# Channel statistics of four image pairs on ScalarE, a later mean over the groups, and a reordered fifth quad in a routed-convolution kernel

## The chip, the cores and the metric

The kernel runs on one core of a Trainium2 chip. The metric is the device time of one execution in microseconds (us), lower is better. The core has TensorE (PE in the profile; its weight loads are PEld), VectorE (DVE), ScalarE (ACT), GpSimd (POOL) and SyncE (SP), which here only issues DMAs. Every engine works through its own instructions in the order in which they are written and waits for the others at semaphores.

## The reference

The input is 32 images of 32 x 32 pixels with 64 channels. Cut to what matters:

```
h = group_norm(x)                          # 32 groups: two channels and all pixels
repeat 3 times:                            # STEPS
    k, v     = h Wk, h Wv                  # two heads of 16
    attn     = softmax over the pixels of (q . k) / 4, per head
    logits   = (sum over pixels of attn * v) Wmlp      # one logit for each of 4 experts
    weights  = softmax(masked logits / 1.5)
    wsel     = the two largest weights, normalised     # the rest are zero
    h_mod    = h * (1 + mean over heads of attn * 1024 * softplus(alpha))
    h        = sum over e of wsel[e] * (conv3x3(h_mod, We[e]) + be[e])
    mask     = without the expert chosen first (the last one stays allowed)
x = x + h
x = x + involution(group_norm(x))          # second layer
```

Since a convolution is linear, the kernel first mixes the experts' weights of an image by `wsel` and then runs one convolution per image.

## The kernel before, in words

Two images stand on the 128 partitions (2 x 64 channels); such a pair is `k`, 0 to 15. Pairs are worked on in **quads** of two pairs, four images: quad `q` = 4p + j, where `p` is the **phase**, 0 to 5, and `j` is 0 to 3. A phase is one step for one half of the batch: phases 0, 2, 4 hold pairs 0 to 7, phases 1, 3, 5 pairs 8 to 15. A quad is convolved in two halves `h` of 16 rows, each with nine taps `t` (`convolve`, L760), four small matmuls a tap; the trace has two records for each of them, 72 a half. From quad 4 on every second quad is **short**: `convolve_short` (L729) works on sums and differences of rows, in four stages of three column taps (24 records a stage). Beside the taps PE runs small jobs at fixed places, by `beside` and `beside_short`: attention maps (L610), scores and values (L552), logits (L598), the permutation of mask and bias (L621), transposes of the input (L523) and `group_average` (L535), a product with `pair_avg` that averages the two channels of a group.

`att` has two units in PSUM. The list `ATT_USES` gives the order of their uses; a use may only start when the use before it in the same unit has been read (`claim`).

**First phase.** Input pairs are transposed into `xin`. VectorE takes the statistics of each (`turned_stats`, L1437 and L1438), `group_average` the mean over a group, `chunk_norm` (L1176 to L1181) the variance, GpSimd the inverse root (L1701, L1704), ScalarE the normalised pair (`normalise`, L913). Chunk 2 is pairs 8 to 11, chunk 3 is pairs 12 to 15; they are not used before phase 1. On GpSimd `row_forms` (L1721 to L1728) follows chunk 3.

**A quad's work beside PE.** ScalarE begins the mixing of the weights (`begin_combine`, L952), VectorE adds the other experts (`combine`, L1402), multiplies the image by 1 + map (`modulate`, L1318), and for a short quad makes row sums (`sum_rows`, L1354 and L1356) and differences (`subtract_rows`, L1370), later the middle rows (`middle_rows`, L1378 and L1379) and the finished rows (`finish_rows`, L1386). ScalarE takes other quads' results out of PSUM (`empty_conv`, L961).

**From quad 6 on** (`GATHER_FROM`) only the two chosen experts are used. `pick_experts` on VectorE (phase 1) or `route_beside` on GpSimd (phases 2 and on) writes their numbers, `top_at`, and signals `top_ready`. SP then loads eight numbers into registers (`chosen_of`, L443) and issues eight DMAs that fetch the two experts of each of the four images (`gather`, L458). `begin_combine(6)` on ScalarE waits for these, `combine_two(6)` (L1423) on VectorE for it. Behind `begin_combine(6)` on ScalarE stands `route_exp(2)` (L924), which starts `route_beside(2)` on GpSimd. Its numbers are for `gather(8)`. Behind `begin_combine(8)` stand the last roundings of the attention of phase 2 (`round_attention`, L988), without which the map of quad 8 can't be made.

`row_max` (L1190), the exponentials (L919) and `weigh` (L1199) are the attention's softmax on VectorE, ScalarE and VectorE. `weigh` reads both units of `att` and so frees the second for the next map.

Of the kernel before, what the change touches and what calls it, by code (L numbers as in the profile page):

```python
# [11 lines left out]
ALU = mybir.AluOpType  # L12
# [4 lines left out]
S = H * W  # L17
# [31 lines left out]
def att_uses():  # L49

    uses = [(0, ("gn", 0)), (0, ("scores", 0)), (1, ("values", 0)), (0, ("logits", 0))]

    def attention_map(q):
        return [(0, ("map", q, 0)), (1, ("map", q, 1))]

    uses += attention_map(0)
    uses += [(0, ("permute", 0))] + [(1, ("turn", 13)), (1, ("turn", 14)), (1, ("turn", 15)), (0, ("gn", 2))]
    uses += attention_map(1) + [(1, ("gn", 3))] + attention_map(2) + attention_map(3) + [(0, ("scores", 1)), (1, ("values", 1))]
    uses += [(0, ("logits", 1))] + attention_map(4)
    for p in range(1, PHASES - 1):  # L60
# [74 lines left out]
def build(nc, A, out):  # L135
    ctx = ExitStack()
    with ctx:
# [3 lines left out]
        def sem(name):  # L141
            return ctx.enter_context(nc.semaphore(name))
# [141 lines left out]
        residual_added = sem("residual_added")  # L284
        final_emptied = sem("final_emptied")
        mv_ready = sem("mv_ready")
        late_mean = sem("late_mean")
        late_mv_ready = sem("late_mv_ready")
        pads_zeroed = sem("pads_zeroed")
# [207 lines left out]
        def _(eng):  # L497
# [150 lines left out]
            def beside(p, j, h, t):  # L648
                at = (j, h, t)
                q = QP * p + j  # L650
                if p == 0:
                    if at == (0, 0, 4):
                        permute(0)
                    elif at in ((0, 0, 3), (0, 0, 5), (0, 0, 7)):
                        turn(12 + t // 2)
                    elif at == (0, 1, 4):
                        group_average(2, chunk(2), CH, mv_ready, 12)
                    elif at == (0, 1, 5):
                        attention_map(1)
                    elif at == (1, 0, 5):  # L660
                        group_average(3, chunk(3), CH, mv_ready, 16)
                    elif at == (1, 1, 2):
                        attention_map(2)
                    elif at == (2, 0, 2):
                        attention_map(3)
                    elif at == (2, 0, 6):
                        attend(1, "scores", sw)
                        attend(1, "values", uw)
                    elif at == (2, 1, 7):
                        logits(1)  # L670
                    elif at == (3, 1, 2):
                        attention_map(4)
# [191 lines left out]

            eng.wait_ge(misc_free, 4)
            eng.wait_ge(late_mv_ready, GP + QP)
            eng.wait_ge(mv_ready, NP + QP)
            nc.tensor.matmul(att[:, 1, 0:2 * GP], pair_avg[:, :], mv[:, GP:NP, :], start=True, stop=True)\
                .then_inc(misc_full, 1)
            for k in range(1, NP):  # L870
# [13 lines left out]
        def _(eng):  # L884
# [92 lines left out]
            def round_attention(p, n):  # L977
# [9 lines left out]
                    eng.wait_ge(reduced, 2 * (p - 1) + n)  # L987
                nc.scalar.activation(parts[:, :], attn[:, :], ACT.Copy).then_inc(parts_ready if n == 2 else rounded, 1)  # L988

            def late_stats(q, n):  # L990

                k, before = slot(q, n), 2 * (q - QP * LAST) + n
                if q in SHORT:
                    eng.wait_ge(residual_added, residuals(q))
                else:
                    eng.wait_ge(final_emptied, final_parts(q, 1))
                part = stats[:, k, 0, 0:1]
                nc.scalar.activation(unused, xin[:, k, :], ACT.Copy, scale=1.0 / (32 * S), accum_out=part).then_inc(late_mean, 1)
                eng.wait_ge(late_mean, before + 1)
                nc.scalar.activation(mv[:, k, 0:1], part, ACT.Copy, scale=32.0)  # L1000
                nc.scalar.activation(unused, xin[:, k, :], ACT.Square, scale=-1.0 / 32, bias=part, accum_out=mv[:, k, 1:2])\
                    .then_inc(late_mv_ready, 1)
                eng.wait_ge(late_mv_ready, before + 1)

            def expanded_weights():

# [28 lines left out]
            for k in (13, 14, 15):  # L1035
                turned(k)
            empty_conv(0, 0)
            normalise(2)
            empty_conv(0, 1)
            begin_combine(2)  # L1040
            empty_conv(1, 0)
            normalise(3)
            empty_conv(1, 1)
# [117 lines left out]
        def _(eng):  # L1161
# [180 lines left out]
                        v.scalar_tensor_tensor(comb[:, 0, n, cols], experts[:, e, cols], wsel[:, 0, QP * n, e:e + 1],  # L1342
                                               comb[:, 0, n, cols], ALU.mult, ALU.add).then_inc(comb_added[n], 1)

            def sum_rows(q):

                w = SHORT.index(q)
                pads = xpad[:, 2 * (q % 2):2 * (q % 2) + 2, :, :]
                modulated(eng, q)
                if w:  # L1350
                    eng.wait_ge(middle_full, 2 * w)
                else:
                    eng.wait_ge(forms_out, 16 * FORMS_WRITTEN)
                v.tensor_tensor(row_sums[:, 0, :, :, :], pads[:, :, 1:H + 1:2, :], pads[:, :, 2:H + 2:2, :], ALU.add)\  # L1354
                    .then_inc(sums_ready, 1)
                v.tensor_tensor(row_sums[:, 1, :, :, :], pads[:, :, 2:H + 2:2, :], pads[:, :, 1:H + 1:2, :], ALU.subtract)\  # L1356
                    .then_inc(sums_ready, 1)

            def subtract_rows(q):

# [29 lines left out]
                eng.wait_ge(rounded, 2 * (p - 1) + n + 1)  # L1390
                v.scalar_tensor_tensor(attn[:, :], parts[:, :], below[:, n:n + 1], attn[:, :], ALU.mult, ALU.add).then_inc(reduced, 1)

            def combine(q):
                p, j = divmod(q, QP)
                cols = slice(0, 4 * ROW if q in SHORT else TAPS * C)
                for e in range(1, K):
                    for n in range(2):
                        if e > 1:
                            eng.wait_ge(comb_added[n], (K - 1) * (2 + q) + e - 1)
# [158 lines left out]
            combine(1)  # L1558
            turned_stats(9)
            turned_stats(10)  # L1560
            turned_stats(11)
            chunk_norm(2)
            eng.wait_ge(norm_done, GP)
            modulate(1)
            turned_stats(12)
            turned_stats(13)
            turned_stats(14)
            turned_stats(15)
            chunk_norm(3)
            combine(2)  # L1570
            modulate(2)
# [6 lines left out]
            shift_logits(1)  # L1578
            reduce_attention(1, 0)
            route(1)  # L1580
            next_mask_and_bias(1)
            reduce_attention(1, 1)
            combine(4)
            modulate(4)
            sum_rows(4)
            permuted(1)
            subtract_rows(4)
            pick_experts(1)

            for p in range(1, PHASES):  # L1590
                for j in range(QP):
# [17 lines left out]
                    if q + 1 < QUADS:  # L1609
# [2 lines left out]
                            shift_logits(p + 1)  # L1612
                        if q == QP:
                            row_max(p + 1)
                        (combine_two if q + 1 >= GATHER_FROM else combine)(q + 1)
                        if j == 0 and attended:
                            if q > QP:
                                row_max(p + 1)
                            weigh(p + 1)
                        if q in SHORT:  # L1620
                            ahead = (0,) if j == 0 or q == QUADS - 2 else (0, 1)
                            modulate(q + 1, ahead)
# [1 line left out]
                            if ahead == (0,):  # L1624
                                modulate(q + 1, (1,))
                            finish_rows(q, 0)
                        if j == 3 and attended:
                            reduce_attention(p + 1, 1)
                            permuted(p + 1)
# [269 lines left out]
```

## Time and profile before

| | us |
|---|---|
| median of 3 runs | 656.03 (655.46 to 656.08) |
| the profiled execution | 655.59 |
| its span, first to last instruction | 653.8 |
| PE busy | 625.2 (96%) |
| DVE busy | 519.5 (79%) |
| ACT busy | 331.1 (51%) |
| POOL busy | 179.3 (27%) |

The profile is of one execution. All starts in the text are us from the start of its span; what lies around the span is 655.59 - 653.8 = 1.8 us. A row of the timeline has start, duration, engine, line, operation, tiles and count; in brackets stands how long the engine was idle before it and what ended that. Several instructions of one line are merged in a row, and its duration then is from the first's start to the last's end. The granted clock of TensorE (PEclk) is a share of its full speed; its mean over the span is 0.982.

### The profile page before, as it was taken

The page shows a single profiled execution, that of the slowest core. Times are in us where ns is not written, and L with a number is a line of the kernel's source. Part 1 is how long each engine was busy: PE and PEld are TensorE (multiplying, and loading weights), DVE is VectorE, ACT ScalarE, POOL GpSimd, SP SyncE. Part 2 cuts the span into 40 slices and gives each one's busy share as a digit, 9 for nine tenths or more (in the row PEclk, how much of TensorE's full clock was granted, in tenths as well). Part 3 has the DMA queues.
Part 4 walks back from the last instruction along what each step waited for, and adds up shares of the span by engine and source line. Part 5 has one row for each costly group of instructions (what it writes and reads, how often), then busy time and mean ns, then how long its engine had stood idle before and what let it go on. Part 6 is the DMA issues. An engine that isn't in the chain of part 4 may idle for free.

```text
span 653.8 us, 15424 instructions
## 1 busy us (share of the span) xinstructions
PE 625.2 (96%) x5984; PEld 257.1 (39%) x5984; DVE 519.5 (79%) x812; ACT 331.1 (51%) x455; POOL 179.3 (27%) x193
## 2 busy tenths in 40 slices
PE   6869999999999999999999999999999999999995
PEld 6533333323343333333333434333444444444442
DVE  5689874998666776775788899869888988888885
ACT  3755443412342143234214756735777887787761
POOL 2100250005500730081028003413432342243230
PEclk9989899999999999999999999998999999999998
DMA  9940030024424243326412642000122221312222
GB/s 323 223 79 2 1 81 7 1 62 109 98 75 97 74 101 94 74 73 151 106 35 66 155 112 74 2 9 10 41 50 56 59 49 41 73 42 49 51 64 65
DMA packets 67461, 47.95 MB, mean 73 GB/s; under 512 B 53602, under 2 KB 54596, under 8 KB 67396
## 3 DMA queue, kind: packets, MB, share of 16 engines
q1 hardware_dynamic: 67108, 46.82, 29.3%
q8 instruction: 47, 0.77, 0.5%
q10 hardware_dynamic: 288, 0.21, 0.1%
q14 instruction: 18, 0.15, 0.1%
HBM read 35.15 MB, written 9.76 MB: 69 GB/s over the span
## 4 chain that ended last, share of the span: by engine, by line
PE 74%; DVE 5%; issue 1%; ACT 0%; DVEq 0%; ACTq 0%
PE conv L760 23%; PE conv L729 14%; PE conv L815 12%; PE att L831 12%; PE att L552 4%; PE att L631 3%; PE att L643 2%; PE att L802 2%; PE att L610 1%; DVE x L1660 1%; DVE xpad L1370 1%; DVE comb L1423 1%; DVE xin L1432 0%; DVE xpad L1318 0%; DVE row_sums L1354 0%
## 5 line engine op out<-in xcount | busy, mean ns | idle before, releaser
L760 PE MATMUL conv<-xpad,comb 64*64 64x512 f32 x2016 | 228.0, 596 | 0.1
L1660 DVE TENSOR_TENSOR x<-conv,x 128x512 f32<-128x512 f32 x288 | 177.9, 683 | 24.1 <-PE conv L815 22.8
L760 PEld LDWEIGHTS conv<-xpad,comb 64*64 64x64 f32 x2016 | 81.6, 134 | 123.9 <-issue 120.5
L815 PE MATMUL conv<-rstack,wse 98*128 98x512 f32 x288 | 95.7, 438 | 1.7 <-DVE xin L1432 0.9
L831 PE MATMUL att<-x,cmp 64*32 64x512 f32 x1280 | 80.5, 601 | 0.0
L815 PEld LDWEIGHTS conv<-rstack,wse 98*128 98x128 f32 x288 | 48.6, 190 | 70.6 <-DVE x L1660 63.9
L1318 DVE SCALAR_TENSOR_TENSOR xpad<-att,x 128x1024 f32<-128x1024 f32 x46 | 54.6, 1218 | 24.2 <-PE att L610 24.0
L961 ACT ACTIVATE x<-conv,bias 128x512 f32<-128x512 f32 x40 | 25.3, 682 | 82.8 <-PE conv L760 82.8
L1812 POOL TENSOR_TENSOR x<-x,xin 128x1024 f32<-128x1024 f32 x15 | 35.9, 2396 | 111.5 <-ACT x L1116 111.5
L952 ACT ACTIVATE comb<-experts,small 128x768 f32<-128x768 f32 (+1 forms) x33 | 27.5, 859 | 77.1 <-PE conv L729 46.8
L729 PE MATMUL conv<-xpad,comb 64*64 64x512 f32 x480 | 56.3, 598 | 1.3 <-DVE x L1379 1.3
L1739 POOL TENSOR_TENSOR rt<-rt 128x16 f32<-128x16 f32 x12 | 5.0, 421 | 190.4 <-ACT rt L924 189.8
L729 PE MATMUL conv<-row_sums,comb 64*64 64x512 f32 x480 | 56.3, 590 | 0.5 <-DVE row_sums L1354 0.5
L1094 ACT ACTIVATE x<-att,small 64x512 f32<-64x512 f32 x64 | 44.1, 689 | 9.5 <-PE att L643 8.9
L1805 POOL TENSOR_TENSOR rstack<-x,rstack 32x1024 fp32r<-32x1024 f32 x16 | 38.2, 2386 | 23.3 <-ACT rstack L1108 23.3
L1116 ACT ACTIVATE x<-att 64x512 f32<-64x512 f32 x60 | 35.6, 593 | 15.1 <-PE att L831 14.0
L1423 DVE SCALAR_TENSOR_TENSOR comb<-experts,small,comb 128x768 f32<-128x768 f32 (+1 forms) x36 | 33.4, 952 | 5.5 <-ACT comb L952 5.3
L729 PEld LDWEIGHTS conv<-xpad,comb 64*64 64x64 f32 x480 | 18.9, 131 | 36.0 <-issue 36.0
L1386 DVE TENSOR_TENSOR x<-x,conv 128x1024 f32<-128x1024 f32 x20 | 24.4, 1218 | 10.6 <-PE conv L729 10.6
L831 PEld LDWEIGHTS att<-x,cmp 64*32 64x32 f32 x1280 | 18.6, 106 | 32.9 <-issue 30.5
L1123 ACT ACTIVATE comb<-att 128x1024 f32<-128x1024 f32 x15 | 15.4, 1027 | 31.0 <-PE att L802 31.0
L729 PEld LDWEIGHTS conv<-row_sums,comb 64*64 64x64 f32 x480 | 18.7, 133 | 30.2 <-issue 28.5
(210 smaller groups left out, 754.1 us busy)
## 6 DMA issues: line engine op xcount, KB each, us to landing
experts<-forms SPq DMA_DIRECT2D x72, 192.0 KB, 3.9
experts<-forms SPq DMA_DIRECT2D x72, 144.0 KB, 2.9
x<-in_x SPq DMA_DIRECT2D x32, 256.0 KB, 5.3
out<-comb SPq DMA_DIRECT2D x30, 256.0 KB, 3.2
rstack<-rstack SPq DMA_DIRECT2D x16, 128.0 KB, 2.3
experts<-in_We SPq DMA_DIRECT2D x1, 1152.0 KB
forms<-experts SPq DMA_DIRECT2D x2, 576.0 KB, 5.7
out<-comb SPq DMA_DIRECT2D x4, 128.0 KB, 2.2
```

Of the source, the lines that this page charges most:

```text
L729: last = nc.tensor.matmul(conv[own[to], h, HW * rows:HW * rows + HW], comb[own[rows], q % 2, n, form * ROW + kw * C:form * ROW + kw * C + ...
L760: last = nc.tensor.matmul(conv[own[to], h, HW * rows:HW * rows + HW], comb[own[rows], q % 2, n, tap(t)], xpad[own[rows], 2 * (q % 2) + n, ...
L815: nc.tensor.matmul(conv[:, unit, cols], wse[:, ORDER[i], :], rstk[s][0:RR, cols], start=True, stop=True).then_inc(exp_full, 1)
L831: last = nc.tensor.matmul(att[q, 0, bank], sum_sel[own_rows, t + upper, :], prod[i][own_rows, cols], start=(r == 0), stop=(r == len(ROUNDS ...
L952: nc.scalar.activation(comb[:, q % 2, n, cols], first, ACT.Identity, scale=weight).then_inc(comb_begun[n], 1)
L1094: done = nc.scalar.activation(xip[s][own[n], 1 + 16 * h:17 + 16 * h, 1:W + 1], att[rows, 1, bank].rearrange("p (a b) -> p a b", b=W), ACT. ...
L1116: nc.scalar.activation(fin[64 * n:64 * n + 64, cols], att[rows, 0, bank], ACT.Copy)\
L1318: v.scalar_tensor_tensor(inner(q, n), img(att[:, use.unit, :]), 1.0, img(x[:, slot(q, n), :]), ALU.add, ALU.mult).then_inc(att_free[use.un ...
L1423: v.scalar_tensor_tensor(comb[:, q % 2, n, cols], chosen[:, n, 1, cols], weight(n, 1), comb[:, q % 2, n, cols], ALU.mult, ALU.add).then_in ...
L1660: v.tensor_tensor(img(prod[i])[:, rows, :], img(conv[:, unit, :])[:, rows, :], xip[s][:, kh + 16 * h:kh + 16 * h + 16, kw:kw + W], ALU.mul ...
L1805: v.tensor_tensor(rstk[s][32:64, :], r64[32:64, :], rstk[s][32:64, :].bitcast(F32), ALU.subtract)\
L1812: v.tensor_tensor(fin, fin, xin[:, k, :], ALU.add).then_inc(fin_ready, 1)
```

## The change

In the first phase the statistics of pairs 12 to 15 move from VectorE to ScalarE (`early_stats`, with a helper that `late_stats` now uses as well), between `empty_conv(0, 0)` and `empty_conv(0, 1)`; the averages of chunk 2 move on PE from tap 4 of quad 0's second half to tap 1 of quad 1; the map of quad 1 comes one tap earlier and no longer stands behind them; on VectorE `modulate(1)` goes ahead of the statistics of pair 11, and on ScalarE `normalise(2)` behind `begin_combine(2)`.

Around the fifth quad (quad 4, the first of phase 1) the next mask and bias go between the two row sums; `weigh(2)` goes behind the first expert's additions of `combine(5)`, in place of behind all three; and `pick_experts(1)` goes from ahead of the quad to behind `finish_rows(4, 0)`.

```diff
@@ att_uses
-    uses += [(0, ("permute", 0))] + [(1, ("turn", 13)), (1, ("turn", 14)), (1, ("turn", 15)), (0, ("gn", 2))]
-    uses += attention_map(1) + [(1, ("gn", 3))] + attention_map(2) + attention_map(3) + [(0, ("scores", 1)), (1, ("values", 1))]
+    uses += [(0, ("permute", 0))] + [(1, ("turn", 13)), (1, ("turn", 14)), (1, ("turn", 15))]
+    uses += attention_map(1) + [(0, ("gn", 2)), (1, ("gn", 3))] + attention_map(2) + attention_map(3) + [(0, ("scores", 1)), (1, ("values", 1))]
@@ tensor, beside
-                    elif at == (0, 1, 4):
+                    elif at == (0, 1, 3):
+                        attention_map(1)
+                    elif at == (1, 0, 1):
                         group_average(2, chunk(2), CH, mv_ready, 12)
-                    elif at == (0, 1, 5):
-                        attention_map(1)
                     elif at == (1, 0, 5):
-                        group_average(3, chunk(3), CH, mv_ready, 16)
+                        group_average(3, chunk(3), CH, early_mv_ready, CH)
@@ scalar
+            def statistics(k, scratch, mean, done, before):
+                part = stats[:, k, 0, 0:1]
+                nc.scalar.activation(scratch, xin[:, k, :], ACT.Copy, scale=1.0 / (32 * S), accum_out=part).then_inc(mean, 1)
+                eng.wait_ge(mean, before + 1)
+                nc.scalar.activation(mv[:, k, 0:1], part, ACT.Copy, scale=32.0)
+                nc.scalar.activation(scratch, xin[:, k, :], ACT.Square, scale=-1.0 / 32, bias=part, accum_out=mv[:, k, 1:2])\
+                    .then_inc(done, 1)
+                eng.wait_ge(done, before + 1)
...
             empty_conv(0, 0)
-            normalise(2)
+            for k in range(NP)[chunk(3)]:
+                early_stats(k)
             empty_conv(0, 1)
             begin_combine(2)
+            normalise(2)
@@ vector, first phase
             turned_stats(10)
+            eng.wait_ge(norm_done, GP)
+            modulate(1)
             turned_stats(11)
             chunk_norm(2)
-            eng.wait_ge(norm_done, GP)
-            modulate(1)
-            turned_stats(12)
-            turned_stats(13)
-            turned_stats(14)
-            turned_stats(15)
             chunk_norm(3)
@@ vector, before quad 4
-            next_mask_and_bias(1)
             reduce_attention(1, 1)
             combine(4)
             modulate(4)
-            sum_rows(4)
+            sum_rows(4, (0,))
+            next_mask_and_bias(1)
+            sum_rows(4, (1,))
             permuted(1)
             subtract_rows(4)
-            pick_experts(1)
@@ vector, the loop over quads
                         if q == QP:
                             row_max(p + 1)
-                        (combine_two if q + 1 >= GATHER_FROM else combine)(q + 1)
-                        if j == 0 and attended:
-                            if q > QP:
+                            combine(q + 1, (1, 2))
+                            weigh(p + 1)
+                            combine(q + 1, (2, K))
+                        else:
+                            (combine_two if q + 1 >= GATHER_FROM else combine)(q + 1)
+                            if j == 0 and attended:
                                 row_max(p + 1)
-                            weigh(p + 1)
+                                weigh(p + 1)
...
                             finish_rows(q, 0)
+                            if q == QP:
+                                pick_experts(p)
```

TensorE in quad 0 and quad 1, before (L535 is the average of a chunk, L610 a map, L760 the convolution's taps, four instructions each):

```order
L760 MATMUL conv<-xpad,comb 64x512 x24
L535 MATMUL att<-mv,wide 128x8
L760 MATMUL conv<-xpad,comb 64x512 x4
L610 MATMUL att<-parts,map_sel 64x512 x8
L760 MATMUL conv<-xpad,comb 64x512 x36
L535 MATMUL att<-mv,wide 128x8
L760 MATMUL conv<-xpad,comb 64x512 x24
```

The same place on TensorE now (the lines have moved by two, L537 for L535 and so on):

```order
L762 MATMUL conv<-xpad,comb 64x512 x20
L612 MATMUL att<-parts,map_sel 64x512 x8
L762 MATMUL conv<-xpad,comb 64x512 x28
L537 MATMUL att<-mv,wide 128x8
L762 MATMUL conv<-xpad,comb 64x512 x16
L537 MATMUL att<-mv,wide 128x8
L762 MATMUL conv<-xpad,comb 64x512 x24
```

The map of quad 1 has moved ahead of the first average, and this average stands 28 instructions later, in quad 1.

VectorE at quad 4 before, from the choice of experts (L1289 to L1296, `small` holds `top_at` and the weights) to the first middle rows (L1378):

```order
L1289 TENSOR_SCALAR cmp<-rt 128x8x4
L1290 TENSOR_SCALAR cmp<-rt 128x8x4
L1291 TENSOR_TENSOR cmp<-cmp,small 128x8x8
L1292 TENSOR_TENSOR cmp<-cmp 128x8x2x2
L1293 TENSOR_TENSOR small<-cmp 128x16
L1295 TENSOR_TENSOR cmp<-cmp,wsel 128x8x8
L1296 TENSOR_REDUCE small<-cmp 128x16
L1190 TENSOR_REDUCE soft<-att 128x1
L1191 TENSOR_SCALAR soft<-soft 128x1
L1402 SCALAR_TENSOR_TENSOR comb<-experts,wsel,comb 128x576 x6
L1199 SCALAR_TENSOR_TENSOR att,soft<-attn,att 128x1024
```

VectorE now, from the additions of two experts (L1419 is L1402 of before, L1215 is L1199, L1334 is L1318, L1395 is L1378, L1403 is L1386, L1305 to L1312 are L1289 to L1296):

```order
L1334 SCALAR_TENSOR_TENSOR xpad<-att,x 128x32x32
L1395 TENSOR_TENSOR x<-x,conv 128x2x16x32
L1396 TENSOR_TENSOR x<-x,conv 128x2x16x32
L1334 SCALAR_TENSOR_TENSOR xpad<-att,x 128x32x32
L1403 TENSOR_TENSOR x<-x,conv 128x2x16x32
L1305 TENSOR_SCALAR cmp<-rt 128x8x4
L1306 TENSOR_SCALAR cmp<-rt 128x8x4
L1307 TENSOR_TENSOR cmp<-cmp,small 128x8x8
L1308 TENSOR_TENSOR cmp<-cmp 128x8x2x2
L1309 TENSOR_TENSOR small<-cmp 128x16
L1311 TENSOR_TENSOR cmp<-cmp,wsel 128x8x8
L1312 TENSOR_REDUCE small<-cmp 128x16
```

The choice of experts now stands behind the middle rows, a modulation and the first finished rows of quad 4.

## Rows read from the trace of the kernel before

**Rows 1.** The page's chain of work that ended last, by engine.
```profile
PE 74%; DVE 5%; issue 1%; ACT 0%; DVEq 0%; ACTq 0%
```

**Rows 2.** Timeline of PE, quads 0 and 1: start, duration, engine, line, count.
```profile
58.45 5.38 PE L760 MATMUL conv<-xpad,comb 64*64 64x512 f32 x48
66.30 0.36 PE L535 MATMUL att<-mv,wide 128*128 128x8 f32 x2 [2.46 <-DVE mv L1438]
```

**Rows 3.** Stretch 67 to 70.5: length, PE busy (count), PEclk, DMA share, GB/s.
```profile
67.00:70.50 3.50, 3.50 (x28) 0.51 0.00 0
```

**Rows 4.** Timeline of DVE, quads 0 to 2.
```profile
61.43 1.42 DVE L1437 BATCH_NORM_STATS2 stats<-xin 128x6 f32<-128x512 f32 x2
...
79.05 7.60 DVE L1402 SCALAR_TENSOR_TENSOR comb<-experts,wsel,comb 128x576 f32<-128x576 f32 x6
86.57 2.34 DVE L1318 SCALAR_TENSOR_TENSOR xpad<-att,x 128x1024 f32<-128x1024 f32 x2
```

**Rows 5.** Timeline of ACT: emptying quad 0, and two pairs' late statistics.
```profile
59.61 1.27 ACT L961 ACTIVATE x<-conv,bias 128x512 f32<-128x512 f32 x2
...
381.81 1.06 ACT L998 ACTIVATE x<-xin 128x1024 f32<-128x1024 f32 x1
...
384.36 1.06 ACT L998 ACTIVATE x<-xin 128x1024 f32<-128x1024 f32 x1
```

**Rows 6.** Timeline of PE, quad 4: values, and the map of quad 5.
```profile
134.24 3.62 PE L552 MATMUL att<-x,uw 128*32 128x512 f32 x32
...
142.19 0.63 PE L610 MATMUL att<-parts,map_sel 64*64 64x512 bf16 x8 [1.60 <-issue]
```

**Rows 7.** Timeline of DVE, quad 4.
```profile
133.71 0.18 DVE L1289 TENSOR_SCALAR cmp<-rt 128x32 f32<-128x32 f32 x1
...
136.43 4.45 DVE L1402 SCALAR_TENSOR_TENSOR comb<-experts,wsel,comb 128x576 f32<-128x576 f32 x6
140.81 1.22 DVE L1199 SCALAR_TENSOR_TENSOR att<-attn,att 128x1024 f32<-128x1024 f32 x1
...
144.59 1.22 DVE L1378 TENSOR_TENSOR x<-x,conv 128x1024 f32<-128x1024 f32 x1 [0.44 <-PE conv L729]
...
148.12 1.21 DVE L1386 TENSOR_TENSOR x<-x,conv 128x1024 f32<-128x1024 f32 x1
```

**Rows 8.** SP's register loads (duration ns, first and last start), 130 to 142.
```profile
L443 SPq TENSOR_LOAD <-small x8: 273/356/467, 134.8 to 139.4; - x8
```

**Rows 9.** Timeline of SP: the DMAs of `gather(6)` and of `gather(8)`.
```profile
141.56 5.61 SPq L458 DMA_DIRECT2D experts<-forms  x8
...
171.35 5.04 SPq L458 DMA_DIRECT2D experts<-forms  x8
```

**Rows 10.** Timeline of ACT, quads 5 and 7.
```profile
150.00 2.01 ACT L952 ACTIVATE comb<-experts,small 128x768 f32<-128x768 f32 x2 [8.88 <-PE conv L729]
153.15 0.23 ACT L924 ACTIVATE rt<-rt 128x32 f32<-128x32 f32 x1 [1.13 <-DVE rt L1245]
...
180.70 0.94 ACT L952 ACTIVATE comb<-experts,small 128x768 f32<-128x768 f32 x1 [2.39 <-DMA experts<-forms]
...
183.94 1.06 ACT L988 ACTIVATE parts<-attn 128x1024 bf16<-128x1024 f32 x1 [1.35 <-DVE attn L1391]
```

**Rows 11.** Timeline of POOL: `top_at` of phase 2.
```profile
165.86 0.20 POOL L1767 CAST small<-cmp 128x16 int32<-128x16 f32 x1
```

**Rows 12.** Timeline of PE: starts of quad 6, of quad 8's map, of quad 8.
```profile
166.15 1.89 PE L729 MATMUL conv<-row_sums,comb 64*64 64x512 f32 x16
...
187.53 0.64 PE L610 MATMUL att<-parts,map_sel 64*64 64x512 bf16 x8
...
193.11 1.07 PE L729 MATMUL conv<-row_sums,comb 64*64 64x512 f32 x8
```

**Rows 13.** Timeline of DVE, quad 5: `combine_two(6)` and its first row sum.
```profile
153.03 1.94 DVE L1423 SCALAR_TENSOR_TENSOR comb<-experts,small,comb 128x768 f32<-128x768 f32 x2
...
158.51 1.29 DVE L1354 TENSOR_TENSOR row_sums<-xpad 128x1088 f32<-128x1088 f32 x1
```

More of the change, by code:

```diff
@@ L286, in build @@
         mv_ready = sem("mv_ready")
+        early_mean = sem("early_mean")
+        early_mv_ready = sem("early_mv_ready")
         late_mean = sem("late_mean")
@@ L866, in _ @@
             eng.wait_ge(late_mv_ready, GP + QP)
-            eng.wait_ge(mv_ready, NP + QP)
+            eng.wait_ge(mv_ready, NP)
             nc.tensor.matmul(att[:, 1, 0:2 * GP], pair_avg[:, :], mv[:, GP:NP, :], start=True, stop=True)\
@@ L988, in round_attention, with early_stats @@
                 nc.scalar.activation(parts[:, :], attn[:, :], ACT.Copy).then_inc(parts_ready if n == 2 else rounded, 1)
+            def statistics(k, scratch, mean, done, before):
[6 more added lines that the diff above has]
+                eng.wait_ge(done, before + 1)
+            def early_stats(k):
+                if k < EARLY:
+                    eng.wait_ge(turn_emptied, k + 1)
+                else:
+                    use = Use("turn", k)
+                    eng.wait_ge(att_free[use.unit], use.freed)
+                statistics(k, x[:, k, :], early_mean, early_mv_ready, k - chunk(3).start)
             def late_stats(q, n):
-                k, before = slot(q, n), 2 * (q - QP * LAST) + n
                 if q in SHORT:
@@ L996, in late_stats @@
                     eng.wait_ge(final_emptied, final_parts(q, 1))
[L997 to L1003, printed above, removed]
+                statistics(slot(q, n), unused, late_mean, late_mv_ready, 2 * (q - QP * LAST) + n)
             def expanded_weights():
@@ L1343, in first_combine, with sum_rows @@
                                                comb[:, 0, n, cols], ALU.mult, ALU.add).then_inc(comb_added[n], 1)
-            def sum_rows(q):
+            def sum_rows(q, forms=(0, 1)):
                 w = SHORT.index(q)
@@ L1353, in sum_rows @@
                     eng.wait_ge(forms_out, 16 * FORMS_WRITTEN)
[L1354 to L1357, printed above, removed]
+                upper, lower = pads[:, :, 1:H + 1:2, :], pads[:, :, 2:H + 2:2, :]
+                if 0 in forms:
+                    v.tensor_tensor(row_sums[:, 0, :, :, :], upper, lower, ALU.add).then_inc(sums_ready, 1)
+                if 1 in forms:
+                    v.tensor_tensor(row_sums[:, 1, :, :, :], lower, upper, ALU.subtract).then_inc(sums_ready, 1)
             def subtract_rows(q):
@@ L1391, in reduce_attention, with combine @@
                 v.scalar_tensor_tensor(attn[:, :], parts[:, :], below[:, n:n + 1], attn[:, :], ALU.mult, ALU.add).then_inc(reduced, 1)
-            def combine(q):
+            def combine(q, upto=(1, K)):
                 p, j = divmod(q, QP)
                 cols = slice(0, 4 * ROW if q in SHORT else TAPS * C)
-                for e in range(1, K):
+                for e in range(*upto):
                     for n in range(2):
@@ L1614, in _ @@
                             row_max(p + 1)
-                        (combine_two if q + 1 >= GATHER_FROM else combine)(q + 1)
-                        if j == 0 and attended:
-                            if q > QP:
+                            combine(q + 1, (1, 2))
+                            weigh(p + 1)
+                            combine(q + 1, (2, K))
+                        else:
+                            (combine_two if q + 1 >= GATHER_FROM else combine)(q + 1)
+                            if j == 0 and attended:
                                 row_max(p + 1)
-                            weigh(p + 1)
+                                weigh(p + 1)
                         if q in SHORT:
```

## The prediction

> **What bounds the kernel now.** I read the chain of waits first. TensorE carries 74% of the span and VectorE 5% [rows 1], so a change pays only where TensorE waits, and costs only where it comes to wait. I then read the timelines of all engines for the first 200 us, in both places that the change touches, and asked of each transfer how early it lands. There are two waits of TensorE to win. One is 2.46 us ahead of the average of chunk 2 [rows 2], and behind it TensorE ran 3.4 us at half its granted clock (0.51 over 67.0 to 70.5 [rows 3]). The other is 1.60 us ahead of the map of quad 5 [rows 6]. One margin is thin: the experts of quad 6. `top_at` is written at 134.8, the eight register loads end near 140, the DMAs start at 141.56 [rows 8, 9], and yet ScalarE's two `begin_combine(6)` instructions, 0.94 each, take 2.01 together from 150.00 [rows 10]. The second started at 151.07, when its weights landed. All times below are on the clock of the profile before; the gain of the first phase is taken off at the end.
>
> **First phase.** TensorE has 48 records in 5.38 us, 0.112 each [rows 2]. Of these 40 come ahead of the map now, so it starts at 58.45 + 4.5 = 62.9. `modulate(1)` begins behind the statistics of pair 10, two pairs at about 1.6 from 61.43 [rows 4], at 64.6, and ends 2.34 later at 66.9. TensorE has done the other 40 records by 63.3 + 4.5 = 67.8, so it isn't held up. The first average now comes with `mv` of pair 11 long ready (66.9 + 1.6 = 68.5 against 69.6). ScalarE starts the four pairs at 59.61 + 1.27 = 60.9 and takes 384.36 - 381.81 = 2.55 for one [rows 5]: done at 71.1. TensorE asks for them at 73.4, which leaves 2.3 us of cover. What is queued behind them on ScalarE, `empty_conv(0, 1)`, ends at 72.4, and quad 1's second half wants it at 76.4.
>
> What is late next is `modulate(2)`. The variance of chunk 3 now comes at 73.4 + 1.3 = 74.7, then `combine(2)` takes 7.60 as before, since GpSimd's `row_forms` still starts at the same distance, and `modulate(2)` 2.3 [rows 4]: 84.6, against 84.8 for TensorE. So the step gives the wait of 2.46 and half of 3.4 us at the full clock, 1.7: **-4.2**. Its bounds are 0 (the statistics late by 2.3 + 4.2) and -4.6 (a little more of the second average's wait).
>
> **Quad 4.** The next mask moves from ahead of `combine(4)` to between the row sums, so VectorE's work up to the permuted mask is the same and TensorE's start of the scores gains 0.2 at most. `weigh(2)` needs the end of the values, 134.24 + 3.62 = 137.86 [rows 6]; it started at 140.81 [rows 7] and now starts at 137.7, so the map of quad 5 finds its unit free and the 1.60 us go. But stage four waits for VectorE's middle rows (L1379). VectorE saves the choice of experts (133.71 to 135.1 [rows 7]), then waits for the scores (134.3) and for the values, and does the same additions: two of the six that take 4.45 ahead of `weigh`, four behind. I count `modulate(5)` for the first images at 142.6 and the middle rows from 143.8 in place of 144.59 [rows 7]. This quad gives **-0.8**, not 2; its bounds are -0.2 and -2.0.
>
> **The choice of experts, moved.** It now stands behind `finish_rows(4, 0)`, which ended at 148.12 + 1.21 = 149.3 and now ends at 148.5. The next steps have no other work in their way:
>
> - From the choice's start to the first register load is 134.8 - 133.71 = 1.1 [rows 7, 8]: 149.6.
> - From `top_ready` to the first DMA is 171.35 - 166.06 = 5.3 [rows 9, 11], which is the eight loads; for quad 6 they ran while `combine(5)` did, and hid: 154.8.
> - From the first DMA to `begin_combine`'s second instruction is 180.70 - 171.35 = 9.35, and for quad 6 151.07 - 141.56 = 9.5 [rows 9, 10]: 164.2, in place of 151.07.
> - ScalarE 0.94, VectorE's second addition 1.0 [rows 13], a clear of 0.1, `modulate(6)` 2.34, first row sum 1.29 [rows 13]: 170.0.
>
> Before, this row sum was ready at 159.8 and TensorE came at 166.15 [rows 12], so 6.4 of 13 us are covered. TensorE, at 165.35 now, waits 4.65, to 170.0. Inside quad 6 it waits some 2 us more: `gather(7)`, its loads and `combine_two(7)` are as late, and the middle rows behind them. Quad 7 starts near 183.4, 6 us behind before.
>
> `route_exp(2)` is queued behind `begin_combine(6)` on ScalarE, and for it waits all of GpSimd's routing of phase 2. It ran at 153.15 and now runs at 165.2. Then 166.06 - 153.15 = 12.9 to `top_ready` [rows 10, 11], 5.3 to the first DMA, 9.35 to the landing: 192.8, in place of 180.70. From there the roundings gave the map's operand at 183.94 + 1.06 = 185.0 [rows 10], so 4.3 later: 197.1. TensorE wants the map of quad 8 at 187.53 + 6 = 193.5 and did it at 187.53 [rows 12]: it starts **+9.6** late. This contains the first wait, for TensorE waits until whichever is later. From quad 8 on the order and the gathers are as before, relative to TensorE, and nothing later gives it back.
>
> Last, the granted clock: an idle stretch of 2.46 us was followed by 3.4 at half [rows 2, 3]; one of 1.60 was not. The two new waits are 4.65 and 3.6. A half clock behind the first falls in quad 6, where TensorE waits for others anyway; one behind the second costs 3.4 / 2 = 1.7. Its bounds are 0 and 3.4; I take **+1.7**.
>
> The Trainium skill, "DMA: Bandwidth & Descriptors", section on latency and other measured facts, gives one register load a floor of about 0.6 us; eight would be an estimate of 4.8 in place of 5.3. By that the two gathers on the path would be 1.0 us sooner.
>
> The **sum**: -4.2 (which includes nothing of quad 4) + 9.6 (which starts from `finish_rows(4, 0)` already 0.8 earlier) + 1.7 = +7.1. Against the profiled execution's 655.59 that is 662.7. The median of the runs is 0.44 above it; I give **662.5**.
>
> **Rivals.**
>
> *The gather is covered.* If the choice's place cost nothing, -4.2 - 0.8 = -5.0 would be left: 650.6, faster. For it speaks that both waits of TensorE really go. Against it speaks that the weights landed 1.07 us after ScalarE asked for them, and that the first DMA can't start ahead of 154.8.
>
> *The second wait is absorbed.* Then quad 7's start decides: +6 - 4.2 = +1.8, 657.4. It would need the numbers of phase 2 to have slack. But `begin_combine(8)` already waited 2.39 for its DMA [rows 10], and the 12 us by which `route_exp(2)` is late exceed what TensorE lost till then by 6.
>
> *The first phase's gain fails*, because ScalarE's statistics come late. From 3.1 us a pair (73.4 - 60.9, by four) TensorE waits for the second average. With one more microsecond a pair nothing but 2.4 is left of the 4.2: 664.3; with none left 666.9. The rows of the late statistics have no gap in which anything else could stand [rows 5]. The Trainium skill, "ScalarE: Activation LUTs", section on table sets, says that a change between functions of different sets costs a table load; between two pairs here, with Copy and Square by turns, 2.55 us leave no room for one.
>
> **How the numbers follow.** The forecast has 0.77, of it 0.5 with the half clock (662.7) and 0.27 without (661.0); the absorbed second wait 0.13; the covered gather 0.07; the failed gain 0.03. Within 0.2% (1.3 us, about what a measurement of this kernel can tell from no change) comes only from the lower edge of the absorbed case, 0.03. So: slower 0.90, same 0.03, faster 0.07. The range reaches from the absorbed case, 657.2, to two stretches of half clock, 664.7.
>
> **What would show it.** Right: no wait ahead of the averages (L537), no half clock near 65; the map of quad 5 without a wait, but a new wait of VectorE's middle rows ahead of stage four; SP's first DMA near 150.6 on the new clock (154.8 - 4.2) and not 137; two waits of TensorE of some 4 us each, ahead of quad 6 and of the map of quad 8, which end in VectorE's row sum and ScalarE's rounding; phases 3 to 5 unchanged but for the shift. Wrong: `begin_combine(6)` within 2 us of its convolution's end; `route_exp(2)` ahead of 155; or a map of quad 8 that starts with no wait, which would put the time near 657.

## The result, and the profile after

The changed kernel is slower: 663.38 us (median of 4 runs, 662.24 to 664.59) against 655.77 for the kernel before, a ratio of 1.0115 with a 95% interval of 1.0103 to 1.0127. The prediction was 662.5.

| | before | after |
|---|---|---|
| profiled execution, us | 655.59 | 664.59 |
| its span, us | 653.8 | 662.8 |
| PE busy, us | 625.2 | 626.6 |
| DVE busy, us | 519.5 | 513.3 |
| ACT busy, us | 331.1 | 340.4 |

VectorE lost 6.2 us of work and ScalarE got 9.3; neither sets the time. Most lines have moved: L535 is L537, L610 is L612, L729 is L731, L1402 is L1419, L1423 is L1440, L924 is L926, L988 is L990, SP's L443 and L458 are L445 and L460.

The page's chain of waits by engine, for the changed kernel; [rows 1] had PE 74% and no SP, GpSimd or DMA in it:

```profile
PE 64%; DVE 7%; SPq 2%; issue 2%; POOL 2%; DMA 1%; ACT 1%; DVEq 0%; ACTq 0%
```

TensorE's longest waits in the changed kernel (line, released by; us in total, times, longest us):

```profile
PE conv L731 <- DVE row_sums L1372: 4.9, 1, 4.9
PE att L612 <- ACT parts L990: 3.7, 1, 3.7
```

The timeline of TensorE has both averages now without a wait, against the 2.46 us of [rows 2]; then the wait ahead of stage four of quad 4, and the two large ones, ahead of quad 6 and of the map of quad 8, with the start of quad 8, to be held against [rows 12]:

```profile
71.31 0.39 PE L537 MATMUL att<-mv,wide 128*128 128x8 f32 x2
...
75.22 0.39 PE L537 MATMUL att<-mv,wide 128*128 128x8 f32 x2
...
120.50 0.61 PE L612 MATMUL att<-parts,map_sel 64*64 64x512 bf16 x8
...
137.63 0.61 PE L612 MATMUL att<-parts,map_sel 64*64 64x512 bf16 x8
...
143.62 2.85 PE L731 MATMUL conv<-xpad,comb 64*64 64x512 f32 x24 [1.04 <-DVE x L1396]
...
167.78 3.64 PE L731 MATMUL conv<-row_sums,comb 64*64 64x512 f32 x16 [4.93 <-DVE row_sums L1372]
...
195.61 1.07 PE L612 MATMUL att<-parts,map_sel 64*64 64x512 bf16 x8 [3.69 <-ACT parts L990]
...
202.64 1.04 PE L731 MATMUL conv<-row_sums,comb 64*64 64x512 f32 x8
```

The granted clock of the changed kernel: the stretch behind the averages is at full clock, and each of the two large waits is followed by about 3.4 us at half (length, PE busy, PEclk, DMA share, GB/s), as the one of [rows 3] was:

```profile
65.00:167.80 102.80, 95.94 (x908) 1.00 0.15 36
167.80:171.30 3.50, 3.50 (x20) 0.51 0.58 165
...
195.00:198.60 3.60, 2.99 (x20) 0.53 0.81 220
```

The chain of waits in order of time (start, duration, what) shows where the 4.9 and 3.7 us come from. It runs from the choice of experts through SP's register loads (L445) and DMA issues (L460), the landing, ScalarE, all of GpSimd's routing, SP again, the landing again, and the roundings, to the map:

```profile
146.56 0.20 DVE small L1309
146.83 0.46 SPq L445
...
152.72 0.57 SPq L460
...
157.55 4.40 DMA experts<-forms
161.97 0.94 ACT comb L954
163.11 0.94 POOL rt L1757
...
175.83 0.21 POOL small L1785
176.06 0.44 SPq L445
...
181.31 0.47 SPq L460
...
185.88 5.27 DMA experts<-forms
191.17 0.94 ACT comb L954
...
194.41 1.06 ACT parts L990
195.61 1.07 PE att L612 x8
```

ScalarE beside it: it stood idle 20.55 us for the experts of quad 6, where its first instruction had waited for the convolution alone [rows 10], and `route_exp(2)` (L926) came right behind, at 162.82 in place of 153.15:

```profile
158.90 0.94 ACT L954 ACTIVATE comb<-experts,small 128x768 f32<-128x768 f32 x1 [20.55 <-DMA experts<-forms]
161.97 0.94 ACT L954 ACTIVATE comb<-experts,small 128x768 f32<-128x768 f32 x1 [2.15 <-DMA experts<-forms]
162.82 0.21 ACT L926 ACTIVATE rt<-rt 128x32 f32<-128x32 f32 x1
```

**The 9.0 us of the two spans, in stretches.** Up to the map of quad 1 the change has moved nothing of weight, yet the profiled execution after has reached 60.42 where that of before had 58.45 [rows 2], 1.97 later; this is the start's clock, not the change (last section). The map of quad 4 comes at 120.50, against 123.03 before: 2.53 earlier, so the first phase gave 4.50. From the map of quad 4 to the map of quad 8 it is 195.61 - 120.50 = 75.11, against 187.53 [rows 12] - 123.03 = 64.50: 10.61 lost. From there to quad 8 it is 7.03 against 5.58, 1.45 lost at half clock. From quad 8 to a wait of 0.87 us near 440 the two are alike, 244.04 against 244.07. The sum is 1.97 - 4.50 + 10.61 + 1.45 = 9.53; the last 0.5 came back behind that wait, 0.4 of it in the last 6 us of the kernel (last section).

### The profile page after: what moved, and what is told of

It is laid out like the page before. It is cut to its first block, busy times and chain, and to the rows that moved or that the text cites. A ratio compares the mean times of both kernels' runs of the same rounds, so it can differ in the third digit from the quotient of the medians.

```text
span 662.8 us, 15438 instructions
## 1 busy us (share of the span) xinstructions
PE 626.6 (95%) x5984; PEld 258.1 (39%) x5984; DVE 513.3 (77%) x800; ACT 340.4 (51%) x475; POOL 179.2 (27%) x193
## 4 chain that ended last, share of the span: by engine, by line
PE 64%; DVE 7%; SPq 2%; issue 2%; POOL 2%; DMA 1%; ACT 1%; DVEq 0%; ACTq 0%
PE conv L762 19%; PE conv L817 12%; PE att L833 11%; PE conv L731 11%; PE att L554 4%; PE att L633 2%; PE att L804 2%; PE att L645 2%; DVE x L1678 2%; DMA experts<-forms 1%; SPq L445 1%; SPq L460 1%; PE att L612 1%; DVE xpad L1387 1%; DVE comb L1440 1%
## 5 line engine op out<-in xcount | busy, mean ns | idle before, releaser
L1334 DVE SCALAR_TENSOR_TENSOR xpad<-att,x 128x1024 f32<-128x1024 f32 x46 | 54.5, 1216 | 19.9 <-PE att L612 19.7
L731 PE MATMUL conv<-row_sums,comb 64*64 64x512 f32 x480 | 57.9, 605 | 4.9 <-DVE row_sums L1372 4.9
L731 PE MATMUL conv<-xpad,comb 64*64 64x512 f32 x480 | 56.4, 598 | 3.1 <-DVE x L1396 3.1
L1440 DVE SCALAR_TENSOR_TENSOR comb<-experts,small,comb 128x768 f32<-128x768 f32 (+1 forms) x36 | 33.5, 955 | 23.9 <-ACT comb L954 23.8
L731 PEld LDWEIGHTS conv<-xpad,comb 64*64 64x64 f32 x480 | 18.9, 131 | 37.8 <-issue 37.8
L731 PEld LDWEIGHTS conv<-row_sums,comb 64*64 64x64 f32 x480 | 19.3, 135 | 35.1 <-issue 33.3
L1403 DVE TENSOR_TENSOR x<-x,conv 128x1024 f32<-128x1024 f32 x20 | 24.3, 1217 | 10.0 <-PE conv L731 10.0
```

What stands on the lines that cost most here:

```text
L731: last = nc.tensor.matmul(conv[own[to], h, HW * rows:HW * rows + HW], comb[own[rows], q % 2, n, form * ROW + kw * C:form * ROW + kw * C + ...
L1334: v.scalar_tensor_tensor(inner(q, n), img(att[:, use.unit, :]), 1.0, img(x[:, slot(q, n), :]), ALU.add, ALU.mult).then_inc(att_free[use.un ...
L1440: v.scalar_tensor_tensor(comb[:, q % 2, n, cols], chosen[:, n, 1, cols], weight(n, 1), comb[:, q % 2, n, cols], ALU.mult, ALU.add).then_in ...
```

## The experiments

Each kernel was timed in rounds with the kernel before on the same chip. The ratios are to it.

### pick_back: the choice of experts back in its old place

```diff
             subtract_rows(4)
+            pick_experts(1)
...
                             finish_rows(q, 0)
-                            if q == QP:
-                                pick_experts(p)
```

> The changed kernel with the choice of experts of phase 1 put back ahead of quad 4's attention; everything else as changed. Theory (the late choice costs, first through the gather of quad 6, then through the routing of phase 2 behind it): both new waits of TensorE (4.93 ahead of quad 6, 3.69 ahead of the map of quad 8) and the half clock behind the second are gone; 655.8 - 4.2 (first phase) - 0.8 (quad 4) = 650.8. Rival (ScalarE's statistics or the order of weigh cost something): clearly above 652. Rival (the place costs nothing): 663.4 as changed.

Measured: 650.28 against 655.57, ratio 0.9920 (0.9908 to 0.9932). Both large waits are gone and no half clock stands between 44 and 640 us. Its TensorE, at the same places:

```profile
118.89 0.61 PE L612 MATMUL att<-parts,map_sel 64*64 64x512 bf16 x8
...
142.00 2.85 PE L731 MATMUL conv<-xpad,comb 64*64 64x512 f32 x24 [1.04 <-DVE x L1396]
...
161.06 1.89 PE L731 MATMUL conv<-row_sums,comb 64*64 64x512 f32 x16
...
182.44 0.64 PE L612 MATMUL att<-parts,map_sel 64*64 64x512 bf16 x8
```

So one move of seven small instructions (about 1.4 us of VectorE) costs 13 us (663.38 - 650.28), and all the other edits together gain 5.3.

### only_late_pick: that move alone, on the kernel before

```diff
             subtract_rows(4)
-            pick_experts(1)
...
                             finish_rows(q, 0)
+                            if q == QP:
+                                pick_experts(p)
```

> The kernel before with the choice of experts alone moved behind the first finished rows of quad 4. Theory: the chain from top_at to the map of quad 8 is as long as in the changed kernel (195.61 - 146.8 = 48.8 us); top_at comes at about 149.7, so the map comes at 198.5 in place of 187.53, + 11.0, and half a clock stretch, 1.7: 655.8 + 12.7 = 668.5. Rival (second wait absorbed): the map starts with no wait, about 662. Rival (gather covered): 655 to 656.

Measured: 667.99 against 655.57, ratio 1.0180 (1.0166 to 1.0195). The first register load is at 150.14 and the map of quad 8 at 198.93, with both waits:

```profile
171.14 3.30 PE L729 MATMUL conv<-row_sums,comb 64*64 64x512 f32 x16 [4.97 <-DVE row_sums L1354]
...
198.93 1.07 PE L610 MATMUL att<-parts,map_sel 64*64 64x512 bf16 x8 [3.65 <-ACT parts L988]
```

The chain is 48.8 us long here too, to the tenth, though all else of the change is missing. The rival that the second wait is absorbed falls.

### route_ahead: ScalarE's order turned round

```diff
                 for j in range(QP):
                     q = QP * p + j
+                    if q == QP + 1:
+                        route_exp(p + 1)
                     if q + 1 < QUADS:
                         begin_combine(q + 1)
...
-                    if p < PHASES - 1 and j == 1:
+                    if p < PHASES - 1 and j == 1 and q > QP + 1:
                         route_exp(p + 1)
```

> The changed kernel with ScalarE's exponential of the routing of phase 2 ahead of begin_combine(6) instead of behind it. Theory (the second wait of TensorE is made by ScalarE's order, since the routing on GpSimd waits behind the gather): the wait of 4.93 ahead of quad 6 stays, the wait of 3.69 ahead of the map of quad 8 and the half clock behind it go: 663.4 - 5.4 = 658.0. Rival (the second wait is made by the gather of quad 7 and SP's own queue): 662 to 663.4, the wait of 3.69 stays within 1 us.

Measured: 658.03 against 655.57, ratio 1.0033 (1.0020 to 1.0047). `route_exp(2)` ran at 148.87, and TensorE has the first wait and not the second:

```profile
166.76 3.69 PE L731 MATMUL conv<-row_sums,comb 64*64 64x512 f32 x16 [4.72 <-DVE row_sums L1374]
...
191.15 0.64 PE L612 MATMUL att<-parts,map_sel 64*64 64x512 bf16 x8
```

So the second wait isn't the gather's own: it is GpSimd's routing, held back by its place in ScalarE's queue. Of the loss behind quad 4, 5.4 us stand behind that one instruction.

### pick_mid: the choice between the two places

```diff
                             combine(q + 1, (2, K))
+                            pick_experts(p)
...
                             finish_rows(q, 0)
-                            if q == QP:
-                                pick_experts(p)
```

> The changed kernel with the choice of experts directly behind combine(5), some 5.8 us earlier than in the changed one and 8.5 later than in pick_back. Theory (a serial chain runs from top_at to the map of quad 8, 48.8 us long, and decides when it ends after TensorE's arrival): no wait ahead of quad 6 beyond 0.5, a wait of about 4 ahead of the map of quad 8, which begins 5.8 earlier than in the changed kernel: 663.4 - 5.8 = 657.6. Rival (what counts is the gather of quad 6 alone, and it is covered here): about 652, with stage four 1.4 later.

Measured: 658.51 against 655.68, ratio 1.0040 (1.0027 to 1.0053). The first wait is covered, the second is not, and the choice's own 1.4 us show ahead of stage four:

```profile
145.24 2.85 PE L731 MATMUL conv<-xpad,comb 64*64 64x512 f32 x24 [2.43 <-DVE x L1396]
...
164.29 1.89 PE L731 MATMUL conv<-row_sums,comb 64*64 64x512 f32 x16
...
190.40 0.63 PE L612 MATMUL att<-parts,map_sel 64*64 64x512 bf16 x8 [3.51 <-ACT parts L990]
```

From the first register load, at 141.3, to the map it is 49.1 us. Counted from the map of quad 4 (120.71 here, 120.50 in the changed kernel) the load came 5.7 earlier, as expected, and the map of quad 8 5.4 earlier, since the chain was 0.3 longer. The expected time kept the half clock behind the second wait, and in this execution it did not come, although TensorE had been idle for 3.51 us:

```profile
190.40:194.00 3.60, 3.60 (x40) 1.00 0.74 217
```

From the map to quad 8 it is 5.58 us, as before the change. So by its trace pick_mid gains 5.4 + 1.45 = 6.9 over the changed kernel, and the two profiled executions are 6.1 apart (of the rest, 0.2 is the start and 0.5 the end). The medians are only 4.9 apart (663.38 to 658.51), where 5.8 were expected. The time is within 1 us of what was expected, but in the one trace kept a term of it is missing; whether the half clock came in the other executions is not shown.

### loads_twice: one term of the chain doubled

```diff
+                if q == GATHER_FROM:
+                    for n in range(2):
+                        for m in range(2):
+                            for r in range(TOP):
+                                eng.value_load(top_at[64 * m:64 * m + 1, p % 2, j + QP * n, r:r + 1], min_val=0, max_val=K - 1)
                 return [eng.value_load(top_at[...
```

> The changed kernel with SP's eight register loads of gather(6) done twice (the first eight values are not used). Theory (the loads stand uncovered on the chain, 5.3 us): the wait ahead of quad 6 grows from 4.9 to 10.1 and everything behind it moves by the same, 663.4 + 5.2 = 668.6. Rival (the loads hide beside the experts' mixing): 663.4.

Measured: 669.27 against 655.68, ratio 1.0204 (1.0188 to 1.0219), 5.9 above the changed kernel. SP's first DMA went from 152.72 to 157.63, by 4.9, and TensorE's waits became:

```profile
PE conv L736 <- DVE row_sums L1377: 9.8, 1, 9.8
...
PE att L617 <- ACT parts L995: 4.0, 1, 4.0
```

The map of quad 8 came at 200.81, 5.2 later. The loads stand in full on the path.

### first_only: the first phase's edits alone

Quad 4 is as in the kernel before; the edit is the diff of the first phase, with `pick_experts(1)` in its old place.

> The kernel before with the first phase's edits alone (statistics of pairs 12 to 15 on ScalarE, averages in the second quad). Theory: the wait of 2.46 us and the half clock of 3.4 us behind it go: 655.8 - 4.2 = 651.6. Rival (the half clock comes anyway, as start-up does, and only the wait goes): 653.3. Rival (statistics late on ScalarE): at 655.8 or above, with a wait ahead of the second average.

Measured: 651.83 against 655.57, ratio 0.9948 (0.9936 to 0.9961), -3.7. The trace sizes it better than the median does: from the first half's tap 5 (58.60 here, 58.45 before [rows 2]) to the map of quad 4 it is 118.68 - 58.60 = 60.08, against 123.03 - 58.45 = 64.58: 4.50 less, as in the changed kernel.

### weigh_only and mask_only: quad 4's two other edits apart

Both are pick_back with one more edit taken back. In weigh_only the mask is back ahead of the reduction:

```diff
             route(1)
+            next_mask_and_bias(1)
             reduce_attention(1, 1)
...
-            sum_rows(4, (0,))
-            next_mask_and_bias(1)
-            sum_rows(4, (1,))
+            sum_rows(4)
```

> pick_back with the next mask and bias back ahead of the last reduction: of quad 4's edits only weigh between the additions of combine(5) is left. Theory (the mask's move brings only the 0.1 to 0.2 by which the permuted mask comes sooner, since VectorE's work up to it is the same): in the profile no wait ahead of the map of quad 5, a wait of about 1 ahead of stage four, stage four at most 0.2 later from the map of quad 4 than in pick_back (there 142.00 - 118.89 = 23.11). Rival (the earlier row sum is what gains): 0.4 or more later.

In mask_only `weigh(2)` is back behind all additions:

```diff
-                            combine(q + 1, (1, 2))
-                            weigh(p + 1)
-                            combine(q + 1, (2, K))
+                            combine(q + 1)
+                            weigh(p + 1)
```

> pick_back with weigh back behind all additions of combine(5): of quad 4's edits only the mask between the row sums is left. Theory: the wait of 1.6 ahead of the map of quad 5 is back, 1.2 to 1.6, and stage four starts 0.7 to 0.9 later from the map of quad 4 than in pick_back (23.11). Rival (the mask's move carries the gain): as pick_back.

The times can't be told from pick_back's: 651.58 (ratio 0.9934, 0.9895 to 0.9974) and 651.86 (0.9942, 0.9920 to 0.9965). The traces can. TensorE of weigh_only, then of mask_only, each from the map of quad 4 to quad 5:

```profile
118.96 0.61 PE L612 MATMUL att<-parts,map_sel 64*64 64x512 bf16 x8
...
142.32 2.85 PE L731 MATMUL conv<-xpad,comb 64*64 64x512 f32 x24 [1.04 <-DVE x L1396]
144.97 1.93 PE L762 MATMUL conv<-xpad,comb 64*64 64x512 f32 x16
```

```profile
119.10 0.61 PE L612 MATMUL att<-parts,map_sel 64*64 64x512 bf16 x8
138.00 0.63 PE L612 MATMUL att<-parts,map_sel 64*64 64x512 bf16 x8 [1.59 <-issue]
...
145.56 1.93 PE L762 MATMUL conv<-xpad,comb 64*64 64x512 f32 x16
```

From the map to quad 5 pick_back takes 144.64 - 118.89 = 25.75, weigh_only 26.01, mask_only 26.46, first_only 145.36 - 118.68 = 26.68. Mask_only did what was expected: the wait of 1.59 is back and quad 5 starts 0.7 later than in pick_back. In weigh_only stage four starts 23.36 behind the map, 0.25 later than in pick_back, which is just over the 0.2 of its theory and short of the rival's 0.4. So the mask's move is worth 0.2 and the move of `weigh` 0.7, although it takes away a wait of 1.6: the other 0.9 come back as the wait of 1.04 ahead of stage four.

### filled: VectorE's idle times used

```diff
             next_mask_and_bias(1)
-            sum_rows(4, (1,))
+            picking = pick_experts(1)        # the numbers, top_at
             permuted(1)
+            sum_rows(4, (1,))
             subtract_rows(4)
-            pick_experts(1)
...
                             combine(q + 1, (1, 2))
+                            picking()        # the weights
                             weigh(p + 1)
```

> pick_back with VectorE's work at quad 4 set in its own idle times: the choice's numbers between the next mask and the permuted mask, the permuted mask ahead of the second row sum, the choice's weights behind the first additions of combine(5). In pick_back TensorE waits 0.80 for the permuted mask and 1.04 ahead of stage four, for VectorE's middle rows. Theory (stage four waits for the sum of VectorE's work and idle times from the row sums on): the scores start 0.5 earlier and the wait ahead of stage four falls to about 0.5, 0.5 faster than pick_back, 649.8. Rival (the order of the two waits only changes): both together stay at 1.8, 650.3.

Measured: 651.08 against 655.68, ratio 0.9930 (0.9916 to 0.9943); not to be told from pick_back. In the trace the wait for the permuted mask fell from 0.80 to 0.47, but the one ahead of stage four stayed:

```profile
118.51 0.61 PE L612 MATMUL att<-parts,map_sel 64*64 64x512 bf16 x8
...
141.36 2.85 PE L731 MATMUL conv<-xpad,comb 64*64 64x512 f32 x24 [1.11 <-DVE x L1400]
```

141.36 - 118.51 = 22.85 against 23.11 in pick_back: 0.26 gained, half of what the theory gave. It sized the mechanism wrong: VectorE's idle times left in pick_back were short already, and from the row sums to the middle rows it works through without a gap in filled. Neither of the two expectations was met.

## Why the prediction was right, point by point

**First phase: -4.2 forecast, -4.50 measured**, twice. No wait ahead of either average, no half clock behind; ScalarE's statistics of four pairs ran from 62.73 to 72.88, 2.54 a pair, 2.3 ahead of the second average at 75.22. The rival of late statistics falls: at 2.54 a pair they were far from its 3.1. The 0.3 more are within what was called "a little more of the second average's wait".

**Quad 4: -0.8 forecast, -0.9 measured** (26.68 to 25.75). The point was that 1.6 us of wait don't make 1.6 us of time: stage four waits for VectorE's middle rows.

**The chain: every link was named, and together they were short by 1.3.** Forecast from the first load to the map: 197.1 - 149.6 = 47.5; measured 48.8. The links, forecast and measured: loads 5.2 and 5.9; first DMA to the second `begin_combine` 9.4 and 9.25; from there to the second set of loads 13.9 and 14.1; loads 5.3 and 5.25; DMA to `begin_combine` 9.35 and 9.86; roundings to the map 4.3 and 4.4. The first loads and the second landing made 1.2 of it. The first set of loads took 5.88 in only_late_pick and in pick_mid too, and the second 5.26, so the 5.3 that the prediction read from `gather(8)` and used for both was too short for `gather(6)`; why the first set takes longer is not shown.

The Trainium skill ("DMA: Bandwidth & Descriptors", section on latency and other measured facts) gives one register load a floor of about 0.6 us; as an estimate, eight at that floor would have made these two links 1.0 shorter together than forecast. Eight took 5.25 and 5.9 here, 0.66 and 0.74 each, which is above the floor, and the trace had the better figure.

**The map of quad 8: +9.6 forecast, +10.6 measured** (-4.50 + 10.61 against -4.2 + 9.6, with quad 4's gain inside both). This is the term that was mis-sized most, and the 1.3 us above are its cause, less 0.3 by which the choice began earlier than forecast.

**The half clock: +1.7 forecast, +1.45 measured**, behind the second wait. The one behind the first (0.51 over 167.8 to 171.3) fell where TensorE waited for others anyway, as forecast: quad 6's middle rows were done at 178.51, and its stage four started at 178.65, still behind a wait of 0.75. In route_ahead the middle rows were done at 177.95 and stage four came right behind. But the prediction could only weigh whether a half clock would come, 0.5 against 0.27, and no length of the wait settles it: it came behind 2.46 us in the kernel before, 3.69 in the changed one and 3.65 in only_late_pick, and did not behind 2.43 and 3.51 in pick_mid. What decides it is open, so that this term came out is in part luck. Without it the changed kernel's time would still have been within the range.

The sum of the mechanism is -4.50 + 10.61 + 1.45 = +7.6. The difference of the medians is 7.6 as well (663.38 - 655.77), but that the two agree to the tenth is luck: the two profiled executions differ by 9.0, with 1.97 of it from the start, which the change does not touch. Against the forecast of +7.1 the errors of the terms (-0.3, +1.0, -0.25) add to about +0.5; they partly cancel.

Three steps of the prediction do not hold as they stand. It put the median at 662.5, below its sum of 662.7, in the same sentence in which it read the median as 0.44 above the profiled execution: by that reading it should have given 663.1. It set TensorE's slack of 6.4 us against the 13 us by which the experts land later; the row sum that TensorE waits for comes only 10.2 later (170.0 against 159.8), and 10.2 - 6.35 + 0.8 is the wait of 4.65 that it states. And two stretches of half clock would put the range's upper end at 664.4 (662.7 + 1.7), not 664.7. None of them touches the mechanism or the wait.

What stays open: the weight of the mask's and of `weigh`'s move is read from one execution each; that these differences repeat is only likely, since pick_back's and first_only's stretches agree with their sum (0.7 + 0.2 against 0.93). filled and pick_back can't be ranked; the best version found is either of them, 0.7 to 0.8% faster than the kernel before.

## What to carry to other kernels

Moving a small step costs not its own length but that of what hangs on it. Ask of each signal it gives which queue takes it up, how long the serial path behind it is (here two register loads of eight, two landings and a routing, 48.8 us) and when its end is wanted: slack read at the first consumer (the row sum of quad 6: 6.4 us, against a delay of 10.2) was not the slack at the second (the map of quad 8: 187.53 - 185.0 = 2.5 us, against a delay of 12.1), whose chain starts behind the first in ScalarE's queue. And a wait taken from the bound engine is worth only the distance to the next thing it would have waited for.

## What the runs showed that was not expected

The same program starts differently from execution to execution. In the profile after, TensorE's clock over 44 to 52 us was 0.57, in the one before 0.79:

```profile
44.00:52.00 8.00, 6.12 (x31) 0.57 0.00 0
```

```profile
44.00:52.00 8.00, 6.80 (x44) 0.79 0.00 0
```

The first of these lines is of the changed kernel. It has 13 matmul records fewer in the same stretch and is 1.97 us late from there on. The work and its waits there are the same in both. The other traces agree: of the eleven kept, the three with 0.57 to 0.59 over this stretch reach the same place in quad 0 at 60.3 to 60.6, the other eight at 58.4 to 59.6. A full clock there gains nothing more: pick_back has 1.00 and comes at 58.80, for it then waits 1.26 us for ScalarE. Executions of one kernel scatter by up to 3.5 us (only_late_pick 666.51 to 670.02, first_only 650.88 to 653.89); that this comes from the start is likely, but only the profiled ones show it. So terms below 1 us have to be read between two marks in the trace, not from medians.

The other difference is at the far end. From the wait of 0.87 us near 440 to the end it is 216.1 us in the changed kernel and 216.6 before. Near 440 the kernel before ran at 0.51 of the clock over 439 to 446, the changed one at 1.00 over 437 to 462. Yet the same group of instructions, 32 records of one line, starts 10.92 us behind that wait before (448.10) and 10.79 in the changed kernel (457.47): 7 us at half clock cost 0.13 there, where VectorE is busy 9.8 of 10 us. The other 0.4 are in the last 6 us, where TensorE's last transposes ran at 0.50 of the clock before and at 1.00 in the changed kernel:

```profile
647.74 1.94 PE L878 MATMUL att<-ident,x 128*128 128x128 f32 x8 [3.10 <-DVE x L1683]
```

```profile
657.13 1.13 PE L880 MATMUL att<-ident,x 128*128 128x128 f32 x8 [3.11 <-DVE x L1701]
```

The first line is of the kernel before, with 6.06 us left to the end, the second of the changed one, with 5.67. pick_back had the full clock near 440 and 1.95 for the last transposes, and takes 216.5.
